# Second copy of theta's high rows: from a ScalarE instruction to a transfer inside SBUF

## What is computed

```python
theta = einsum('bchw,kc->bkhw', x, theta_w)            # 32 rows
phi   = pool2(einsum('bchw,kc->bkhw', x, phi_w))       # 32 rows, 256 columns after 2x2 max pooling
beta  = softmax(theta^T phi)                           # 1024 x 256 per image
g     = pool2(einsum('bchw,kc->bkhw', x, g_w))         # 128 rows, 256 columns
x     = gamma * (o_w @ (g @ beta^T)) + x
```

## Time and profile before

| | |
|---|---|
| median of three runs | 295.62 us |
| the profiled execution | 296.33 us |
| its span | 294.6 us |
| TensorE (PE) busy | 283.1 us, 96% |
| VectorE (DVE) busy | 239.1 us, 81% |
| ScalarE (ACT) busy | 236.3 us, 80% |
| GpSimd (POOL) busy | 114.4 us, 39% |
| mean granted TensorE clock | 0.994 of full speed |
| from the scores of one image to those of the next, in the loop | about 17 us |

### The profile page before, as it was taken

How to read it: one execution, slowest core, us unless ns; L and a number is a source line. 1 busy time by engine, 2 the same in 40 slices (tenths; PEclk the granted TensorE clock), 3 DMA queues, 4 the chain that set the end, 5 groups by cost and what they waited for, 6 DMA issues and landing times.

```text
span 294.6 us, 4343 instructions
## 1 busy us (share of the span) xinstructions
PE 283.1 (96%) x1286; PEld 225.5 (77%) x1286; DVE 239.1 (81%) x402; ACT 236.3 (80%) x518; POOL 114.4 (39%) x57
## 2 busy tenths in 40 slices
PE   7888799999998999999999999999999999999995
PEld 5465687888777788788878887788878788787884
DVE  5987878888896878979788887979888797978750
ACT  3687778897977989787988979787897879799752
POOL 6052334534443353335345344435435333633300
PEclk9999799999999999999999999999999999999999
DMA  7623508365470846638083664708374471817033
GB/s 247 172 39 56 182 9 239 125 204 170 157 214 3 234 139 187 185 129 218 36 232 128 198 174 157 215 40 213 118 216 156 158 214 77 217 78 219 13 143 142
DMA packets 12617, 44.56 MB, mean 151 GB/s; under 512 B 2033, under 2 KB 2623, under 8 KB 11360
## 3 DMA queue, kind: packets, MB, share of 16 engines
q1 hardware_dynamic: 12252, 44.13, 51.3%
q10 hardware_dynamic: 276, 0.20, 0.2%
q0 software_dynamic: 80, 0.13, 0.1%
HBM read 17.37 MB, written 16.78 MB: 116 GB/s over the span
## 4 chain that ended last, share of the span: by engine, by line
PE 84%; DVE 6%; DMA 3%; SPq 2%; ACT 2%; issue 2%; ACTq 0%; DVEq 0%
PE psV L647 15%; PE psV L649 14%; PE psV L648 14%; PE psY L671 9%; PE psY L647 6%; PE psY L648 6%; PE psY L649 6%; PE psX L710 4%; PE psV L757 4%; PE psZ L710 2%; DMA x_raw<-x 2%; PE psZ L724 2%; PE psX L724 2%; SPq L253 2%; PE psY L757 1%
## 5 line engine op out<-in xcount | busy, mean ns | idle before, releaser
L315 POOL TENSOR_TENSOR prob_lo<-prob,prob_hi 128x1024 fp32r<-128x1024 f32 x30 | 71.9, 2396 | 109.0 <-ACT prob_hi L379 109.0
L309 POOL TENSOR_TENSOR x_lo<-x_raw,x_hi 128x1024 fp32r<-128x1024 f32 x15 | 36.1, 2410 | 50.7 <-DVE x_hi L473 42.1
L365 ACT ACTIVATE psX<-psX,neg_max 128x256 f32<-128x256 f32 x64 | 28.5, 446 | 26.5 <-DVE neg_max L542 26.5
L357 ACT CAST theta_aug<-thetaphi 32x512 fp32r<-32x512 f32 x64 | 39.6, 618 | 2.6 <-DVE thetaphi L490 1.5
L647 PE MATMUL psV<-prob_hi,value_hi 128*128 128x512 f32 x94 | 38.3, 407 | 0.0
L649 PE MATMUL psV<-prob_hi,value_lo 128*128 128x512 f32 x94 | 37.4, 398 | 0.0
L648 PE MATMUL psV<-prob_lo,value_hi 128*128 128x512 f32 x94 | 37.2, 396 | 0.0
L490 DVE TENSOR_TENSOR thetaphi<-psY,thetaphi_rest 64x512 f32<-64x512 f32 x32 | 21.8, 682 | 11.8 <-ACT thetaphi_rest L351 11.7
L365 ACT ACTIVATE psZ<-psZ,neg_max 128x256 f32<-128x256 f32 x64 | 29.6, 481 | 0.0
L560 DVE TENSOR_TENSOR theta_aug<-psZ,own_tile 16x512 fp32r<-16x512 f32 x32 | 20.5, 678 | 11.1 <-PE psZ L717 11.1
L496 DVE TENSOR_TENSOR theta_aug<-thetaphi,theta_aug 32x512 fp32r<-32x512 f32 x32 | 26.0, 814 | 1.0
(11 more groups left out here) (113 smaller groups left out, 729.2 us busy)
## 6 DMA issues: line engine op xcount, KB each, us to landing
x_raw<-x SPq DMA_DIRECT2D x15, 1024.0 KB, 5.5
out<-y SPq DMA_DIRECT2D x15, 1024.0 KB, 4.0
x_edge<-x_hi SPq DMA_DIRECT2D x64, 104.0 KB
x_edge<-x_lo SPq DMA_DIRECT2D x32, 104.0 KB
x_raw<-x SPq DMA_DIRECT2D x4, 256.0 KB, 4.1
out<-y SPq DMA_DIRECT2D x4, 256.0 KB, 2.0
band_rev<-ring SPq DMA_DIRECT2D x2, 128.0 KB, 3.9
proj_raw<-proj_wT ACTq DMA_DIRECT2D x1, 192.0 KB, 3.8
```

The costliest lines, as they stand in the source:

```text
L309: nc.gpsimd.tensor_tensor(x_lo[:, par, :, cols], x_raw[:, par, :, cols], x_hi[:, par, :, cols].bitcast(F32), ALU.subtract).then_inc(x_lo_r ...
L315: nc.gpsimd.tensor_tensor(prob_lo[:, h], prob[:, h], prob_hi[:, h].bitcast(F32), ALU.subtract).then_inc(prob_lo_ready, 1)
L357: nc.scalar.copy(theta_aug[rows, par, h * HALF:(h + 1) * HALF], thetaphi[0:K, h, :]).then_inc(theta_hi_ready, 1)
L365: last = nc.scalar.activation(tiles[:, t, :], tiles[:, t, :], ACT.Exp, bias=neg_max[:, col:col + 1], accum_out=exp_sum[:, col:col + 1])
```

## The change

The ScalarE list loses the second `theta_high` instruction of each half, for every image but the first. SyncE gets, for each half, a wait for the high rows and one transfer from partitions 0-31 of `theta_aug` to partitions 32-63 (32 partitions x 2 KB, 64 KB). TensorE's `scores` gets one more wait, for that transfer (for the first image: for ScalarE's copy). `theta_low` waits for the high rows alone. In SyncE's body the order becomes: the two theta transfers, the load of the image after next, the six edge transfers, the store.

```diff
+        first_theta_copy_ready = sem("first_theta_copy_ready")
+        theta_copied = [sem("theta_copied0"), sem("theta_copied1")]
...
+            def copy_theta_high(i, par, h):
+                sp.wait_ge(theta_hi_ready, upto(2, i, par, h + 1))
+                cols = slice(h * HALF, (h + 1) * HALF)
+                sp.dma_start(theta_aug[K:2 * K, par, cols].bitcast(F32),
+                             theta_aug[0:K, par, cols].bitcast(F32)).then_inc(theta_copied[h], 16)
+
             def image(i, par):
                 if has_next(i, par):
-                    x_edges(*following(i, par))
+                    for h in range(2):
+                        copy_theta_high(*following(i, par), h)
                 if has_next_but_one(i, par):
 
                     for h in range(2):
                         sp.wait_ge(x_lo_ready[h], upto(1, i, par, 1))
                     load(i + 1, par)
+                if has_next(i, par):
+                    x_edges(*following(i, par))
...
             def theta_high(i, par, h):
 
                 act.wait_ge(thetaphi_summed, upto(2, i, par, h + 1))
-                for rows in (slice(0, K), slice(K, 2 * K)):
-                    nc.scalar.copy(theta_aug[rows, par, h * HALF:(h + 1) * HALF],
-                                   thetaphi[0:K, h, :]).then_inc(theta_hi_ready, 1)
+                cols = slice(h * HALF, (h + 1) * HALF)
+                nc.scalar.copy(theta_aug[0:K, par, cols], thetaphi[0:K, h, :]).then_inc(theta_hi_ready, 1)
+                if is_first(i, par):
+                    nc.scalar.copy(theta_aug[K:2 * K, par, cols], thetaphi[0:K, h, :]).then_inc(first_theta_copy_ready, 1)
...
             def theta_low(i, par, h):
                 cols = slice(h * HALF, (h + 1) * HALF)
-                dve.wait_ge(theta_hi_ready, upto(4, i, par, 2 * h + 2))
+                dve.wait_ge(theta_hi_ready, upto(2, i, par, h + 1))
...
             def scores(i, par, h):
 
                 pe.wait_ge(theta_lo_ready, upto(2, i, par, h + 1))
+                if is_first(i, par):
+                    pe.wait_ge(first_theta_copy_ready, h + 1)
+                else:
+                    pe.wait_ge(theta_copied[h], 16 * upto(1, i, par, 0))
                 pe.wait_ge(phi_ready, upto(1, i, par, 1))
```

## The result

The changed kernel takes 323.45 us (median of 4 runs, 322.24 to 325.99) where the one before takes 295.61; the ratio is 1.096, its 95% interval 1.089 to 1.103. The forecast was 323. The profiled execution took 322.24 us with a span of 320.4, so 25.9 more than the profiled one of before.

What follows compares the result with a forecast made beforehand. TensorE, busy 283.1 of 294.6 us, was taken as the bound. Terms 28.0 + 0.7 - 0.6 - 1.0 = +27.1 us on the profiled 296.33 gave 323.4; the median 322.7, stated as 323, range 312 to 336.

Steps and rivals of the forecast that it cites:

- ScalarE starts prob of half 1 1.09 us earlier, prob_low then leads theta_low by 0.14: Half 1 of each image: GpSimd's prob_low, formerly 0.95 us behind theta_low's start, would start 0.14 us ahead.
- theta_low is held until 0.55 after GpSimd's end, 2.13 late: VectorE's theta_low of half 1 would wait for the shared port, ending at 155.60 in place of 153.47.
- The idle time of ScalarE gives nothing back, and the delay goes on to L717: ScalarE's 1.69 us idle ends with VectorE's maxima, so shift_parts, which TensorE's L717 awaits, comes 2.13 us late too.
- 2.0 per image: TensorE in images 3 to 16: 2.13 less 0.1 to 0.2 us lost each; +28.0 us for 14 images.
- The start, -0.6: Image 2: ScalarE's second theta instruction leaves the chain of waits just ahead of prob, saving 0.6 us.
- image 2, +0.7: Image 2: TensorE at half clock covers part of the delay; between 0 and 2.0 us, taken as +0.7.
- The late load, -1.0: Sync queue: the load goes ahead of the edges, saving a 0.83 us TensorE wait and a few tenths nearby; -1.0 us.
- The clock: Rival: stalls also make TensorE's clock fall, 1.2 us each; 340 us if in all 14 images, 331 in half; chance 0.24.
- its likeliest case: GpSimd takes the port ahead of VectorE's theta_low, with TensorE at full clock; chance 0.55.
- The transfers cost nothing: Both theta transfers on SP would land in 2.0 to 2.76 us, before the scores need them; no cost.
- The added wait on TensorE: Ahead of half 0's scores: 0.05 to 0.1 us, hidden by the delays; uncovered, up to +0.7 to +1.5 in all.
- The rival in which VectorE keeps the port: Half 1: theta_low takes its 0.68 us and prob_low ends a little later; 294.7 us, chance 0.14.

Runs made afterwards that it cites:

- e1: Changed kernel, transfers kept, but ScalarE again runs a second theta instruction of each half, into a spare tile nobody reads; 295.14 us.
- e4: Changed kernel with one small ScalarE instruction (32 x 64, into a spare tile) ahead of the exponentials of half 1; 293.55 us.
- e2: Changed kernel without theta transfers or waits for them, later images' second high rows not refreshed; 321.86 us.
- e3: Changed kernel, but GpSimd's prob_low of half 1 also waits for theta_low of half 1; 293.40 us.
- e6: Kernel before the change, with only the load moved ahead of the six edge transfers; 294.77 us, ratio 0.997.
- e9: Changed kernel with prob_low of half 1 waiting for theta_low, and the load issued ahead of the theta transfers as well; 356.39 us.

## Why the prediction was right

**Where the time went.** Busy time between the scores of image 3 and those of image 16, before and then after, 13 images each:

```profile
49.90:271.79 221.89, 220.53 (x1028) 177.87 (x1028) 188.64 (x313) 188.54 (x417) 93.48 (x39) 1.00 0.55 160
```

```profile
49.73:295.75 246.02, 227.07 (x1027) 176.74 (x1028) 215.10 (x313) 171.42 (x390) 93.13 (x40) 0.99 0.53 152
```

That is +24.1 us; up to there -0.2, and behind it (294.6 - 271.79 = 22.8, 320.4 - 295.75 = 24.7) +1.8: together 25.8.

- *ScalarE starts prob of half 1 1.09 us earlier, prob_low then leads theta_low by 0.14.* It leads by 0.12. e1 and e4 show that this lead is the cause, e2 that it is enough.
- *theta_low is held until 0.55 after GpSimd's end, 2.13 late.* It is: from L520's start to theta_low's end are 3.23 us, before 1.13, so 2.10.
- *The idle time of ScalarE gives nothing back, and the delay goes on to L717.* So it is in the rows above. Of the delay 1.27 us show before the scores (19.0 in 15 waits), where 1.45 were forecast.
- *2.0 per image.* This term was too large. From the undisturbed pair of images at 164 to 202 us the pitch is 18.81, before (153 to 187) 16.97: 1.84. I had let the shift matmul come 0.1 to 0.2 later at no cost, since its weight load ended 0.13 before it. It starts 0.05 after `shift_parts` is ready, so the whole distance of before, less 0.05, was slack: 160.42 to 160.78 gives 0.31, and one image later 177.43 to 177.69 gives 0.21. Their mean is 0.26, and 2.10 less 0.26 is 1.84. 14 x 1.84 is 25.8 in place of 28.0.
- *The start, -0.6, and image 2, +0.7.* The scores of image 2 begin at 30.90 in place of 31.50; by image 3 the gain is down to 0.17, so image 2 lost 0.4. That this is near 0.7 is luck. The term took image 2 to run at half clock, as in the earlier trace rows, and so to cover part of the delay. But the changed kernel's clock stayed up there:

```profile
32.00:34.00 2.00, 0.77 (x6) 0.48 (x5) 1.97 (x2) 0.00 (x0) 0.93 (x1) 1.00 1.07 389
```

From the scores of image 2 to those of image 3 it takes 18.83 us, and e3, also at full clock, 17.06: the delay cost 1.8. About 1.3 of it was hidden by the fall that the kernel before had there.

- *The late load, -1.0.* The wait of the earlier trace rows is gone; the images around it had cost 1.3, and e6 gains 1.3 at equal clock.
- *The clock.* This rival came true in part. In the profiled execution the clock fell once:

```profile
147.00:149.00 2.00, 2.00 (x8) 1.62 (x7) 2.00 (x3) 0.65 (x3) 0.00 (x0) 0.52 0.90 139
149.00:151.00 2.00, 2.00 (x8) 1.54 (x7) 1.93 (x5) 2.00 (x8) 0.00 (x0) 0.63 0.81 119
```

It followed the stall before the scores of half 1, 1.37 us in that image, and the image took 20.2 us, some 1.3 over the others. The other images of the loop had the same stall, 1.13 to 1.38 us, and kept the clock. The other three runs granted 0.978 to 0.989 where this one granted 0.995, and took 1.2 to 3.8 us more. So the median of 323.45 is 1.2 above the profiled execution, where the forecast put it 0.7 below (323.4 and 322.7). The agreement to half a microsecond is partly luck: the sum was 2.2 too high for the images, and had no clock falls in its likeliest case.

- *The transfers cost nothing.* They land in 2.0 us (taken: 2.0 to 2.76), and TensorE never waits for one. The added wait on TensorE doesn't show here either, as forecast: e2, without it, has the same time per image.

The rival in which VectorE keeps the port was priced at 294.7; e3, which makes it so, measured 293.4, with the clock up in all its runs.

## What to carry to other kernels

Relieving an engine that isn't on the chain moves what it feeds: before taking work from it, list what starts earlier and which instruction of the critical engine that start would now precede. Where GpSimd reads SBUF and VectorE reads two tiles of it, a quarter of a microsecond in their order of starts decided over 2 us here, so fix the order with a wait instead of leaving it to timing. A wait placed in a DMA queue delays all that stands behind it, and a small transfer close behind a large one lands late: price both before moving anything in the queue. And compare variants at equal granted clock, or a fall in some of the runs hides or feigns a gain of 1 to 2 us.

## What the runs showed of the hardware

VectorE's instruction with two SBUF inputs and GpSimd's exclude each other for one whole instruction: 2.79 in place of 0.68 us when GpSimd leads by 0.12, 1.70 when GpSimd's work is cut in two, 0.68 with GpSimd at 2.81 when VectorE leads by 0.14. That confirms over a full overlap what the Trainium skill, "SBUF — State Buffer", section "Who interferes with whom", states, and that the trace of before had shown for the last 0.4 us only. A 64 KB transfer inside SBUF lands in 2.0 us with no load close ahead of it, and in 5.6 us (median of e9) where most of them go out 2.4 to 4.1 us behind a load of 1 MB that itself follows a store of 1 MB on the same queue. In the profiled execution of the kernel before the granted clock fell to half at 31.6 us, just after a pause of TensorE of 1.61 us; 25 of the 47 runs of that kernel beside the experiments granted 0.994 or less. The length of the pause alone doesn't decide it. In e2 TensorE paused for 1.77 us at the same place and the clock stayed up:

```profile
32.00:34.00 2.00, 2.00 (x14) 1.78 (x13) 1.97 (x4) 0.00 (x0) 2.00 (x1) 1.00 0.16 25
```

In the changed kernel it fell after one of 1.37 us and not after its neighbours of the same length.
